# A graph-attention layer on one core: the first feed-forward product of each tile with the rows as weights, and its result turned back by TensorE

## The chip, the cores and the metric

One core of a Trainium2 chip runs the whole layer. The metric is the device time of one execution in microseconds. Five engines work in order of their own instructions and wait for each other on semaphores: TensorE (PE in the rows, its weight loads PEld), VectorE (DVE), ScalarE (ACT), GpSimd (POOL) and SyncE (SP).

## The reference, cut to what matters

`x` has 4096 rows of 512, and 131072 edges join them. The middle part, attention over the edges of each row, is computed by code that the change leaves as it is.

```python
def _ln(x, g, b): ...                     # layer norm
z = _ln(x, ln1_g, ln1_b)
att = _sparse_attention(z, row_index, col_index, att_bias, Wq, bq, Wk, bk, Wv, bv, Wo, bo)
x = x + att
z = _ln(x, ln2_g, ln2_b)
ff = jax.nn.silu(z @ W1 + b1) @ W2 + b2   # W1: 512 x 1024, W2: 1024 x 512
return x + ff                             # then one more norm of input + this
```

## The kernel before, in words

The first phase (about 1.9 ms of the profiled span) sorts the edges into records, computes q, k and v for all rows, and stores them. The second phase, where the change is, walks over 32 tiles of 128 rows (loop `tiles`, variable `t`). The edges of a tile are cut into groups of 8 per row, at least three groups per tile, 145 in all. GpSimd gathers the k and v rows of a group by eight indirect DMAs (L521) into a ring of three buffers, and SyncE passes their arrival on.

Each group goes through the engines as a pipeline. VectorE multiplies q and k (`products`, L991). TensorE sums the products by transposing matmuls (`sum_d`, L1321), adds up the v sums of the group before (`turn_sum`, L1349), and turns the scores (`turn_scores`, L1329, after ScalarE's copy in `take_scT`, L676). VectorE takes the maximum and subtracts it (`softmax`, L1037 to L1041), ScalarE takes the exponents (L687). The v rows are then weighed, half by ScalarE (`weigh`, L703: pair 3 of the group before ahead of the exponents, pair 0 behind them, with the copy `take_vT`, L682, in its middle) and half by VectorE (L1002). TensorE sums them (`sum_v`, L1339).

The order of instructions is written out by hand. The first three groups of a tile are stages 0, 1 and 2 on TensorE and VectorE, and all later groups share a loop, stage 3. ScalarE has one body for the first group (`body(t, None)`) and one for all others (`body(t, i)`). The feed-forward work of earlier tiles is threaded into these stages:

- TensorE, behind `sum_v(3)`: stage 0 has both halves of the second product, `down(oldest, 0)` and `down(oldest, 1)` (L1389), stage 1 has `up(older, 0)` (L1379) and `turn_att` (L1356), and stage 2 has `up(older, 1)` and the output projection `out_proj` (L1364). `turn_z2` (L1370) stands at the head of stage 1.
- ScalarE: `hidden(k, 0)` in the second group and `hidden(k, 1)` in the third, eight instructions each (L725 and L726 in turn).
- VectorE: `silu` (L1049) of half 0 in stage 2 and of half 1 in stage 0; the norm `middle` in stage 0 and the last norm in stage 2.

`up` makes the hidden layer already turned: W1 is the weight operand, 128 hidden units at a time, and the turned rows z2T stream through it, 128 columns. The result has a hidden unit on each partition, so b1 is one number per partition, and ScalarE adds it as the bias of its activations; and hT can at once be the weight operand of `down`. Each float32 matmul that is no transpose shows as two MATMUL records, so one half of `up` (16 matmuls) is 32 records and one half of `down` (4 matmuls of 512 columns) is 8 records. The hidden halves lie in the PSUM banks h_ps[0] and h_ps[1].

Of the kernel before, what the change touches and what calls it, by code (L numbers as in the profile page):

```python
# [14 lines left out]
P = 128  # L15
# [20 lines left out]
def layer_kernel(nc, x, src, dst, edge_bias, Wq, bq, Wk, bk, Wv, bv, Wo, bo, ln1_g, ln1_b,  # L36
# [30 lines left out]
    bias_rows = nc.dram_tensor("bias_rows", [3, 3 * C], BF16, kind="Internal").ap()  # L67
# [6 lines left out]
    with ExitStack() as ctx:  # L74
# [39 lines left out]
        def part(words):  # L114
# [14 lines left out]
        bias_c, bias_f, bias_r = (part(3 * KT).rearrange("p (w k) -> p w k", w=3) for _ in range(3))  # L129
        bias_cut = part(9 * KT // 2).bitcast(BF16).rearrange("p (i w k) -> p i w k", i=3, w=3)  # L130
# [27 lines left out]
        hT = part(HID)  # L158
        prods = part(GROUP * C).rearrange("p (s c) -> p s c", s=GROUP)
        vw = part(GROUP * C).rearrange("p (s c) -> p s c", s=GROUP)  # L160
        scT_sb, vT_sb = part(2 * P), part(C)
        assert max(used_sort, pos_c[0]) <= REGION_C
# [18 lines left out]
        b1_col = sb("b1_col", [P, HT])  # L181
        b1_half = sb("b1_half", [P, HT])
# [44 lines left out]
            att_sb wo_done z2_ready z2_turned z2_sb h_done0 h_done1 h_act0 h_act1 h_ready0 h_ready1 y_done y_taken out_ready out_sent consts_c  # L227
# [6 lines left out]
        H_DONE = [S["h_done0"], S["h_done1"]]  # L234
        LANDED = [S[f"landed{pair}"] for pair in range(PAIRS)]
# [28 lines left out]
        def _(sp):  # L264
# [10 lines left out]
            for w, b in enumerate((bq, bk, bv)):  # L275
                sp.dma_start(bias_c[:, w, :], b.rearrange("(p k) -> p k", p=P)).then_inc(S["weights_loaded"], 16)
            for to, b in ((bo_all, bo), (b2_all, b2)):
                sp.dma_start(to, b.rearrange("(a n) -> a n", a=1).broadcast_to([P, C])).then_inc(S["weights_loaded"], 16)
            with nc.allow_non_contiguous_dma(reason="vectors of a few KB to columns"):
# [3 lines left out]
                sp.dma_start(b1_col[:, :], b1.rearrange("(k p) -> p k", p=P)).then_inc(S["weights_loaded"], 16)  # L283
# [10 lines left out]
            with nc.allow_non_contiguous_dma(reason="pieces of three vectors, once"):  # L294
                sp.wait_ge(S["bias_cut"], 1)
                for w in range(3):
                    sp.dma_start(bias_rows[:, w * C:(w + 1) * C].rearrange("i (p k) -> p i k", p=P), bias_cut[:, :, w, :]).then_inc(S["bias_out"], 16)
# [4 lines left out]
            sp.wait_ge(S["bias_out"], 48)  # L302
            sp.dma_start(bias_bf, bias_rows).then_inc(S["bias_in"], 16)
# [297 lines left out]
        def _(act):  # L601
# [56 lines left out]
            act.mul(b1_half[:, :], b1_col[:, :], 0.5).then_inc(S["phase1_act"], 1)  # L658
            act.drain()
# [57 lines left out]
            def hidden(k, a):  # L717
# [56 lines left out]
            for a in range(2):  # L774
                hidden(NT, a)
# [718 lines left out]
```

## Time and profile before

| | |
|---|---|
| median of 3 timed runs | 3778.58 us (3778.52 to 3779.97) |
| span of the profiled execution, first to last instruction | 4385.0 us |
| second phase in it, 1900 to 4310 us | 2410 us, 145 groups |
| granted TensorE clock in it | 0.92 of full, against 0.65 in the first phase |
| share of the DMA engines in it | 0.72, 240 GB/s |

The profiled execution is 606 us (16%) longer than the timed ones, and the page gives no time for it beside its span. Durations of single instructions are read from it, and waits with caution. A group is measured here on TensorE, from the first L1329 row of one group to the first of the next.

### The profile page before, as it was taken

How to read it: one execution, taken by the hardware profiler on the slowest of the kernel's cores; microseconds unless marked ns; L12 is line 12 of the kernel's file. 1: busy time of each engine (PE TensorE's matmuls, PEld its weight loads, DVE VectorE, ACT ScalarE, POOL GpSimd, SP SyncE). 2: the span in 40 equal slices, each digit the busy share in tenths (PEclk: the TensorE clock that was granted, in tenths of full speed). 3: DMA queues.
4: the chain of work that ended last, by engine and by line, in shares of the span. 5: the costliest groups of instructions: out<-in, count | busy, mean ns of one | idle time of the engine just before them, and what ended most of it. 6: DMA issues, size and time to landing. Idle time of an engine off the chain costs nothing.

```text
span 4385.0 us, 82363 instructions
## 1 busy us (share of the span) xinstructions
PE 2962.7 (68%) x18693; PEld 2259.3 (52%) x18694; DVE 2634.4 (60%) x6428; ACT 1724.8 (39%) x6427; POOL 2648.6 (60%) x2550
## 2 busy tenths in 40 slices
PE   7444554455455455547778788888888888888888
PEld 5222222222222232236667676776767777677676
DVE  8555555455555555536567566666666666666665
ACT  0011111111111111125666565665666666566664
POOL 0255555555556555567667666666667667666662
PEclk5566666666666666668889999998999999999999
DMA  6222222222222222266667777777677777777762
GB/s 230 70 61 61 61 61 61 57 65 61 61 64 64 59 61 63 59 226 229 225 227 263 242 233 256 242 240 252 221 246 249 246 235 244 246 238 247 240 218 77
DMA packets 285667, 719.24 MB, mean 164 GB/s; under 512 B 86899, under 2 KB 103475, under 8 KB 285382
## 3 DMA queue, kind: packets, MB, share of 16 engines
q0 software_dynamic: 211776, 585.54, 40.9%
q1 hardware_dynamic: 73862, 133.41, 9.7%
q14 instruction: 22, 0.18, 0.0%
q8 instruction: 7, 0.11, 0.0%
HBM read 717.02 MB, written 72.97 MB: 180 GB/s over the span
## 4 chain that ended last, share of the span: by engine, by line
PE 37%; issue 18%; DVE 17%; another core or an unknown queue 14%; ACT 5%; DVEq 4%; POOL 2%; ACTq 1%; DMA 1%; POOLq 1%; PEld 0%; SPq 0%; PEldq 0%
PE bank L1321 10%; PE wide L1379 6%; PE wide L1339 6%; PE bank L1389 5%; ACT region_c L703 4%; DVE region_c L938 3%; DVE region_c L903 3%; PE bank L1278 2%; DVE region_c L914 2%; PE bank L1364 2%; DVE region_c L918 2%; PE bank L1220 2%; PE wide L1265 1%; DVEq L900 1%
## 5 line engine op out<-in xcount | busy, mean ns | idle before, releaser
L521 POOL DMA_INDIRECT region_a<-kv,cols x1160 | 1405.5, 1212 | 490.7 <-issue 451.2
L408 POOL DMA_INDIRECT records<-region_c,pos_i x1024 | 999.4, 976 | 895.9 <-DVE pos_i L921 588.5
L703 ACT ACTIVATE region_c<-region_a,pr 128x64 f32 x4640 | 1157.3, 337 | 96.1 <-remote 60.7
L991 DVE TENSOR_TENSOR region_c<-region_a,region_c 128x1024 f32 x580 | 674.4, 1221 | 233.4 <-issue 174.2
L1321 PE MATMUL bank<-ident,region_c 128*128 128x128 f32 x4640 | 614.1, 288 | 145.8 <-DVE region_c L991 89.1
L1321 PEld LDWEIGHTS bank<-ident,region_c 128*128 128x128 f32 x4640 | 581.4, 197 | 176.2 <-issue 163.8
L1339 PE MATMUL wide<-ident,region_c 128*128 128x128 f32 x4640 | 600.6, 287 | 67.3 <-ACT region_c L703 44.0
L1339 PEld LDWEIGHTS wide<-ident,region_c 128*128 128x128 f32 x4640 | 553.9, 151 | 96.5 <-ACT region_c L703 63.1
L914 DVE TENSOR_TENSOR region_c<-wide,region_c 128x512 f32<-128x512 f32 x128 | 136.3, 1065 | 700.3 <-remote 468.5
L1265 PE MATMUL wide<-region_c 64*128 64x64 f32 x2048 | 193.7, 345 | 461.8 <-issue 438.6
L1278 PE MATMUL bank<-region_b,region_a 128*128 128x512 f32 x768 | 495.9, 803 | 6.5 <-issue 6.1
L1265 PEld LDWEIGHTS wide<-region_c 64*128 64x128 f32 x2048 | 175.6, 251 | 551.6 <-issue 543.5
L1379 PE MATMUL wide<-region_c,region_b 128*128 128x128 f32 x2048 | 298.4, 303 | 107.7 <-issue 104.4
L1002 DVE TENSOR_TENSOR region_c<-region_a,pr 128x1024 f32<-128x1024 f32 x290 | 341.7, 1219 | 8.2 <-remote 6.7
L1379 PEld LDWEIGHTS wide<-region_c,region_b 128*128 128x128 f32 x2048 | 279.5, 217 | 120.4 <-issue 116.3
L1278 PEld LDWEIGHTS bank<-region_b,region_a 128*128 128x128 f32 x768 | 191.1, 262 | 273.1 <-issue 273.1
L647 ACT ACTIVATE region_a<-bank 128x512 f32<-128x512 f32 x96 | 57.3, 597 | 634.0 <-remote 419.5
L903 DVE SCALAR_TENSOR_TENSOR region_c<-region_a,region_c 128x128 bf16<-128x128 int16 x1024 | 291.7, 350 | 24.3 <-issue 24.3
L1389 PE MATMUL bank<-region_b,region_c 128*128 128x512 f32 x512 | 237.6, 607 | 21.6 <-issue 21.6
L676 ACT COPY region_c<-bank 128x256 f32<-128x256 f32 x145 | 53.9, 372 | 482.0 <-PE bank L1321 342.1
L1285 PE MATMUL bank<-ident,region_a 128*128 128x128 f32 x128 | 35.7, 434 | 289.5 <-DVE region_a L935 281.3
L1220 PE MATMUL bank<-region_c 128*64 128x64 bf16 x2048 | 189.8, 317 | 61.2 <-issue 34.3
(184 smaller groups left out, 3189.3 us busy)
## 6 DMA issues: line engine op xcount, KB each, us to landing
region_a<-srcT SPq DMA_DIRECT2D x128, 256.0 KB
region_a<-kv,cols POOLq DMA_INDIRECT x1160
region_a<-hiT SPq DMA_DIRECT2D x256, 64.0 KB
x_rows<-region_c SPq DMA_DIRECT2D x32, 512.0 KB
records<-region_c,pos_i POOLq DMA_INDIRECT x1024
kv<-region_a SPq DMA_DIRECT2D x32, 512.0 KB
records<-region_c SPq DMA_DIRECT2D x32, 480.0 KB, 14.8
region_a<-in_x_dram SPq DMA_DIRECT2D x32, 256.0 KB
```

The lines of the kernel that those rows point to most:

```text
L408: pool.indirect_dma_start(records, bass.IndirectOffsetOnAxis(ap=pos_i[j % 2][:, s:s + 1], axis=0), rec_w[j % 2][:, s, :], None).then_inc(S ...
L521: pool.indirect_dma_start(KV[r][:, s, :], None, kv, bass.IndirectOffsetOnAxis(ap=cols[r][:, s:s + 1], axis=0), bounds_check=L - 1, oob_is_ ...
L703: last = act.activation(vw[:, s, of], v_part[:, s, C + hd * D:C + (hd + 1) * D], ACT.Copy, scale=pr[:, s + 1, hd:hd + 1])
L903: last = dve.scalar_tensor_tensor(eq[:, s * P:(s + 1) * P], srcb[b][:, s * P:(s + 1) * P], src_f[:, bass.ds(st * STREAMS + s, 1)], tri[:, ...
L991: last = dve.tensor_tensor(prods[:, of, :], kv_in[:, of, 0:C], q.unsqueeze(1).broadcast_to([P, 2, C]), ALU.mult)
L1002: dve.tensor_tensor(vw[:, s:s + 2, :].rearrange("p s (h d) -> p s h d", h=HEADS), kv_in[:, s:s + 2, C:2 * C].rearrange("p s (h d) -> p s h ...
L1265: last = pe.matmul(wide_ps[b][:, side, s * LO:(s + 1) * LO], hitT[b][rows, s * P:(s + 1) * P], table_sb[rows, s * LO:(s + 1) * LO], start= ...
L1278: last = pe.matmul(qkv_ps[w][:, :], zT1[:, c * P:(c + 1) * P], Wqkv[:, w, c, :], start=False, stop=c == KT - 1)
L1321: last = pe.matmul(scT_ps[:, a * P:(a + 1) * P], prod_cols[:, i, a * SH:(a + 1) * SH], ident[:, :], start=i == 0, stop=i == D // FOLD - 1, ...
L1339: last = pe.matmul(vT_ps[:, c * P:(c + 1) * P], vw[:, s, c * P:(c + 1) * P], ident[:, :], start=s == 0 and c == 0, stop=s == GROUP - 1, is ...
L1379: last = pe.matmul(h_ps[m // 4][:, (m % 4) * P:(m % 4 + 1) * P], W1_sb[:, c, m * P:(m + 1) * P], z2T[:, c * P:(c + 1) * P], start=c == 0, ...
L1389: last = pe.matmul(y_ps[:, :], hT[:, m * P:(m + 1) * P], W2_sb[:, m, :], start=m == 0, stop=m == HT - 1)
```

## The change

`up` takes the turned rows z2T as weights, 128 at a time, and W1 streams through in 512 columns, so a half is 4 matmuls. The result has the rows on the partitions and the hidden units along the free axis. The bias b1 now varies along the free axis: it is cut into three bf16 rows whose sum is exactly b1, in the first phase beside the other biases, and enters by one more matmul with a bf16 weight of ones, three rows deep. ScalarE handles a half in two instructions of 512 columns (a halving copy, and tanh) instead of eight of 128. VectorE's `silu` is as before. Since `down` needs the hidden units on the partitions, TensorE turns each half by four transposes into the same PSUM bank (`turn_hidden`), and ScalarE copies it out. Two stages of semaphores are new: `h_turned` and `hT_sb`. `down` waits for `hT_sb` instead of `h_ready`.

```diff
 # ScalarE
-                for c in range(HT // 2):
-                    ps = h_ps[a][:, c * P:(c + 1) * P]
-                    half_b = b1_half[:, a * HT // 2 + c:a * HT // 2 + c + 1]
-                    act.activation(hT[...], ps, ACT.Identity, bias=half_b, scale=0.5)
-                    last = act.activation(ps, ps, ACT.Tanh, bias=half_b, scale=0.5)
-                last.then_inc(H_ACT[a], 1)
+                act.activation(hid[:, a * HID // 2:(a + 1) * HID // 2], h_ps[a][:, :], ACT.Copy, scale=0.5)
+                act.activation(h_ps[a][:, :], h_ps[a][:, :], ACT.Tanh, scale=0.5).then_inc(H_ACT[a], 1)
+            def turn_hidden(k, a):
+                act.wait_ge(H_TURNED[a], k)
+                act.copy(hT[:, a * HID // 2:(a + 1) * HID // 2], h_ps[a][:, :]).then_inc(HT_SB[a], 1)
...
                 weigh(0, at, now, t, i is None)
+                if i is None:
+                    with act.If(t > 2):
+                        turn_hidden(act.snap(older), 0)
+                        turn_hidden(act.snap(older), 1)
 # TensorE
-                for m in range(a * HT // 2, (a + 1) * HT // 2):
-                    for c in range(KT):
-                        last = pe.matmul(h_ps[m // 4][:, (m % 4) * P:(m % 4 + 1) * P], W1_sb[:, c, m * P:(m + 1) * P],
-                                         z2T[:, c * P:(c + 1) * P], start=c == 0, stop=c == KT - 1)
+                of = slice(a * HID // 2, (a + 1) * HID // 2)
+                pe.matmul(h_ps[a][:, :], ones_bf[:, :], b1_rows[:, of], start=True, stop=False)
+                for c in range(KT):
+                    last = pe.matmul(h_ps[a][:, :], z2T[:, c * P:(c + 1) * P], W1_sb[:, c, of], start=False, stop=c == KT - 1)
                 last.then_inc(H_DONE[a], 1)
+            def turn_hidden(k, a):
+                pe.wait_ge(H_READY[a], k)
+                for c in range(HT // 2):
+                    last = pe.transpose(h_ps[a][:, c * P:(c + 1) * P], hid[...], ident[:, :])
+                last.then_inc(H_TURNED[a], 1)
             def down(k, a):
-                pe.wait_ge(H_READY[a], k)
+                pe.wait_ge(HT_SB[a], k)
...
                         with pe.If(t > 2):                    # stage 0, behind sum_v(3)
                             pe.reg_add(oldest, oldest, 1)
-                            down(pe.snap(oldest), 0)
+                            turn_hidden(pe.snap(oldest), 1)
                     with pe.If(t > 2):
-                        down(pe.snap(oldest), 1)
+                        down(pe.snap(oldest), 0)
...
                 if stage == 1:                                # behind sum_v(3)
+                    with pe.If(t > 2):
+                        down(pe.snap(oldest), 1)
                     with pe.If(t > 1):
                         up(pe.snap(older), 0)
...
                         out_proj(t)                           # stage 2
+                    with pe.If(t > 1):
+                        turn_hidden(pe.snap(older), 0)
```

In the first phase SyncE issues one more small DMA out to `bias_rows` and one more in (the load of b1 itself is only laid out otherwise), VectorE's seven instructions that cut the biases work on 20 columns instead of 12, and ScalarE's halving of b1 is gone. Behind the loop the last three tiles get the same steps written out.

## Rows read from the trace of the kernel before

**Rows 1.** The page: span, and busy time of each engine.
```profile
span 4385.0 us, 82363 instructions
PE 2962.7 (68%) x18693; PEld 2259.3 (52%) x18694; DVE 2634.4 (60%) x6428; ACT 1724.8 (39%) x6427; POOL 2648.6 (60%) x2550
```
**Rows 2.** The page: the chain that ended last, share by engine.
```profile
PE 37%; issue 18%; DVE 17%; another core or an unknown queue 14%; ACT 5%; DVEq 4%; POOL 2%; ACTq 1%; DMA 1%; POOLq 1%; PEld 0%; SPq 0%; PEldq 0%
```
**Rows 3.** PE's timeline, a stage 0: start, length, line; idle before in brackets.
```profile
3280.99 0.63 PE L1329 MATMUL bank<-fold,region_c 128*128 128x32 f32 x4 [0.46 <-ACT region_c L676]
...
3285.74 7.03 PE L1389 MATMUL bank<-region_b,region_c 128*128 128x512 f32 x16
3292.61 0.60 PE L1370 MATMUL bank<-ident,region_c 128*128 128x128 f32 x4
...
3297.71 0.63 PE L1329 MATMUL bank<-fold,region_c 128*128 128x32 f32 x4 [0.46 <-ACT region_c L676]
```
**Rows 4.** PE's timeline, a stage 1.
```profile
3369.98 3.74 PE L1379 MATMUL wide<-region_c,region_b 128*128 128x128 f32 x32
3373.55 0.60 PE L1356 MATMUL bank<-ident,region_c 128*128 128x128 f32 x4
...
3378.65 0.63 PE L1329 MATMUL bank<-fold,region_c 128*128 128x32 f32 x4 [0.46 <-ACT region_c L676]
```
**Rows 5.** Stretches: length; busy of PE, PEld, DVE, ACT, POOL; clock; DMA share; GB/s.
```profile
1900.00:4310.00 2410.00, 1933.46 (x13198) 1657.10 (x13199) 1546.82 (x2777) 1463.41 (x5646) 1638.09 (x1506) 0.92 0.72 240
3281.00:3297.70 16.70, 15.71 (x92) 11.40 (x92) 14.23 (x32) 10.34 (x40) 13.04 (x13) 1.00 0.83 288
3365.20:3378.70 13.50, 12.47 (x109) 12.05 (x109) 10.35 (x16) 11.58 (x45) 10.41 (x10) 1.00 0.66 200
4263.70:4280.50 16.80, 15.67 (x112) 13.01 (x112) 12.01 (x24) 11.03 (x44) 12.25 (x13) 1.00 0.93 335
```
**Rows 6.** VectorE's timeline in the stage 0 of Rows 3.
```profile
3289.46 4.63 DVE L991 TENSOR_TENSOR region_c<-region_a,region_c 128x1024 f32 x4 [0.37 <-issue]
```
**Rows 7.** Groups in 1900:4300: busy us, mean ns; idle before, releasers.
```profile
L1379 PE MATMUL wide<-region_c,region_b 128*128 128x128 f32 x1856 | 276.0, 306 | 104.6 <-issue 104.4
L1389 PE MATMUL bank<-region_b,region_c 128*128 128x512 f32 x464 | 216.5, 609 | 21.6 <-issue 21.6
L1364 PE MATMUL bank<-region_b,region_c 128*128 128x512 f32 x240 | 115.8, 627 | 0.0
L725 ACT ACTIVATE region_c<-wide,b_half 128x128 f32<-128x128 f32 x232 | 88.5, 382 | 26.2 <-PE wide L1379 20.9 <-remote 5.2
L726 ACT ACTIVATE wide<-wide,b_half 128x128 f32<-128x128 f32 x232 | 83.2, 358 | 0.0
```
**Rows 8.** The first phase's bias matmul (L1276): duration ns min, median, max.
```profile
L1276 PE MATMUL bank<-region_c,ones_bf x96: 384/602/605, 172.2 to 1880.8; 3*128 3x512 bf16 x96
```
**Rows 9.** ScalarE's timeline in a stage 2 that nothing disturbs.
```profile
4267.57 0.26 ACT L687 ACTIVATE pr<-sc 128x72 f32<-128x72 f32 x1
...
4269.99 0.56 ACT L682 COPY region_c<-wide 128x512 f32<-128x512 f32 x1
4270.46 2.02 ACT L703 ACTIVATE region_c<-region_a,pr 128x64 f32 x8
```
**Rows 10.** PE's timeline after a long idle stretch.
```profile
3024.93 1.06 PE L1329 MATMUL bank<-fold,region_c 128*128 128x32 f32 x4 [2.69 <-ACT region_c L676]
3025.80 6.38 PE L1339 MATMUL wide<-ident,region_c 128*128 128x128 f32 x32
```
**Rows 11.** Stretches: the one of Rows 10.
```profile
3024.90:3032.20 7.30, 7.27 (x38) 7.28 (x39) 5.23 (x7) 6.08 (x25) 2.55 (x2) 0.56 0.38 151
```
**Rows 12.** ScalarE's timeline in the stage 0 of Rows 3.
```profile
3285.33 2.02 ACT L703 ACTIVATE region_c<-region_a,pr 128x64 f32 x8 [0.23 <-issue]
3292.82 0.58 ACT L682 COPY region_c<-wide 128x512 f32<-128x512 f32 x1 [5.48 <-remote]
```
**Rows 13.** Stretches: a disturbed stage 2.
```profile
3447.20:3473.10 25.90, 20.09 (x112) 17.33 (x112) 12.84 (x27) 11.07 (x44) 15.44 (x17) 0.80 0.76 264
```

More of the change, by code:

```diff
@@ L66, in layer_kernel @@
     row_key = nc.dram_tensor("row_key", [L], F32, kind="Internal").ap()
-    bias_rows = nc.dram_tensor("bias_rows", [3, 3 * C], BF16, kind="Internal").ap()
+    bias_rows = nc.dram_tensor("bias_rows", [3, 3 * C + HID], BF16, kind="Internal").ap()
     q_rows = nc.dram_tensor("q_rows", [L, C], F32, kind="Internal").ap()
@@ L128, in layer_kernel @@
         bias_bf = part(3 * C // 2).bitcast(BF16)[0:3, :]
-        bias_c, bias_f, bias_r = (part(3 * KT).rearrange("p (w k) -> p w k", w=3) for _ in range(3))
-        bias_cut = part(9 * KT // 2).bitcast(BF16).rearrange("p (i w k) -> p i w k", i=3, w=3)
+        bias_c, bias_f, bias_r = (part(3 * KT + HT) for _ in range(3))
+        bias_cut = part(3 * (3 * KT + HT) // 2).bitcast(BF16).rearrange("p (i k) -> p i k", i=3)
         bo_all, b2_all, xb_row = part(C), part(C), part(2 * C)
@@ L157, in layer_kernel @@
         s_all, z2 = part(2 * C), part(C)
-        hT = part(HID)
+        hid = part(HID)
+        hT = hid
         prods = part(GROUP * C).rearrange("p (s c) -> p s c", s=GROUP)
@@ L161, in layer_kernel @@
         scT_sb, vT_sb = part(2 * P), part(C)
+        b1_rows = part(HID // 2).bitcast(BF16)[0:3, :]
+        assert used_sort <= pos_c[0] - HID // 2
         assert max(used_sort, pos_c[0]) <= REGION_C
@@ L768, in _ @@
             take_vT()
+            for a in range(2):
+                turn_hidden(NT - 2, a)
             turn_z2(NT - 1)
@@ L772, in _ @@
             hidden(NT - 1, 1)
+            for a in range(2):
+                turn_hidden(NT - 1, a)
             turn_z2(NT)
@@ L775, in _ @@
                 hidden(NT, a)
+            for a in range(2):
+                turn_hidden(NT, a)
         @block.vector
@@ L878, in _ @@
             dve.drain()
-            dve.tensor_copy(bias_cut[:, 1, :, :], bias_r)
+            dve.tensor_copy(bias_cut[:, 1, :], bias_r)
             dve.drain()
-            dve.tensor_copy(bias_f, bias_cut[:, 1, :, :])
+            dve.tensor_copy(bias_f, bias_cut[:, 1, :])
             dve.drain()
@@ L1456, in _ @@
             turn_sum()
+            turn_hidden(NT - 2, 1)
             down(NT - 2, 0)
@@ L1463, in _ @@
             out_proj(NT)
+            turn_hidden(NT - 1, 0)
+            turn_hidden(NT - 1, 1)
             down(NT - 1, 0)
@@ L1468, in _ @@
             up(NT, 1)
+            turn_hidden(NT, 0)
+            turn_hidden(NT, 1)
             down(NT, 0)
```

33 lines of the change are left out of this document (17 added, 16 removed).

## The prediction, as put on record before the changed kernel was run

> **What bounds the kernel now.** I read the page first for which engine is busy: TensorE, with 68% of the span, and no other above 60% [rows 1]. The chain that ended last runs mostly through TensorE, then through waits that the profile calls issue, and VectorE [rows 2]. An average doesn't say what one more microsecond on TensorE costs, so I read the timeline of single groups. In a stage 0, from one L1329 row to the next (16.72 us), TensorE goes from `sum_v` into both halves of `down` without a gap, 6.87 us from 3285.74 to 3292.61, and from there into `turn_z2` [rows 3]. In a stage 1, `up(0)` takes 3.57 us and `turn_att` follows at once; the group is 13.4 us long [rows 4]. TensorE is busy 15.71 of 16.70, 12.47 of 13.50 and 15.67 of 16.80 us in undisturbed stages 0, 1 and 2 [rows 5]. So in these three stages TensorE's own queue is the bound, and feed-forward work put into it moves the next group's scores by nearly its own length. VectorE is the next limit in stage 0 only: its products end at 3289.46 + 4.63 = 3294.1, some 3.6 us ahead of the next L1329 [rows 3, 6]. The gathers have room: 0.72 of the DMA engines over the phase, though up to 0.93 in single stages [rows 5].
>
> **TensorE's instructions.** `up` before: 32 records in 3.57 us per half [rows 4]. After: 8 records of 512 columns. `down` has the same form and takes 6.87 / 2 = 3.44 us per half [rows 3]; so the columns cost what they cost, four times as many in a fourth of the records, and only 0.13 us go. The bias matmul is 512 columns of bf16. It appears only in the first phase, with a shortest record of 384 ns [rows 8]. A float32 record of 512 columns is 609 ns long [rows 7] at a pace of 430 ns, so 180 ns of a record overlap the next; that leaves 0.2 us (bounds: 0, fully overlapped, and 0.6, its longest record). `turn_hidden` is 4 transposes; `turn_z2` of the same form takes 3293.05 - 3292.61 = 0.44 us (its end is the next start, and I take the same for `turn_att`). Per tile: 2 x (3.44 + 0.2 - 3.57) + 2 x 0.44 = +1.0 us, bounds 0.6 to 1.8.
>
> Here the Trainium skill speaks for a better exchange. "TensorE: Matmul & The Clock Gate", section "Back-to-back issue gap", gives sustained 81 ns for a matmul of 128 columns and 131 ns for one of 512, that is 0.40 of the time for the same columns. By that the new `up` would cost 2 x 0.4 x 3.57 = 2.9 us instead of 6.9, and the sum below would be some 116 us (29 x 4.0) lower, about 3845 us and still slower than before. The trace disagrees: 430 ns against 3.57 / 32 = 112 ns [rows 3, 4], a ratio of 3.9, no saving in kind.
>
> **What moves on TensorE.** `down(1)` leaves stage 0 and goes to stage 1. Stage 1 was bound by TensorE, so it grows by 3.44 + 0.07 = 3.5 us. Stage 2 grows by `turn_hidden(0)` and the bias, 0.44 + 0.07 = 0.5 us. `turn_hidden(0)` waits for `silu(0)`, which VectorE does ahead of the scores of stage 2, so it doesn't stall.
>
> Stage 0 loses 3.44 us of `down(1)` and has 0.44 of `turn_hidden(1)`, but `down(0)` now waits for a copy by ScalarE. ScalarE issues that copy behind `weigh(0)`, and that stands behind the exponents of this same group, which need TensorE's own scores of this group. From the L1329 row of an undisturbed group (4263.7, the start of the last stretch of rows 5): exponents at 4267.57, that is +3.9, `take_vT` at +6.3, its second eight L703 end at 4270.46 + 2.02, +8.8 [rows 5, 9]. The copy is like L682, 0.56 us [rows 9]: +9.3, with the branch and the semaphore +9.5. TensorE is through with `sum_v` at +4.75 (3285.74 - 3280.99) and with the turn at +5.2 [rows 3]: it stands idle for 4.3 us. `down(0)` then ends at +12.95, where both halves ended at +11.62 before: stage 0 grows by 1.3 us although half its feed-forward work left. Queued behind the waiting `down(0)` on TensorE are `turn_z2` and `sum_d` of the next group, for which ScalarE and then VectorE wait. Bounds of this term: -1.0 (if the copy came in time, VectorE would hold the group, with the 3.6 us of rows 6 less the 2.5 us that `sum_d`, copy and scores take behind it) and +1.3.
>
> **The clock.** A gap on TensorE has a second price. Behind the 2.69 us gap at 3024.93, 32 records of L1339 took 6.38 us, where 32 of L1379 with the same shape take 3.74 [rows 4]; the granted clock in that stretch is 0.56, that is, mostly the 1.2 GHz level instead of 2.4 [rows 10, 11]. I looked at all 28 gaps over 2 us in the second phase: 26 of them are followed by work that is 1.2 to 3.3 us late, and the eight over 3 us by 2.4 us on average. I take 2.3 us per tile; bounds 0 and 3.4 (all of `down(0)` at half pace).
>
> **The other engines.** ScalarE had 16 instructions of L725 and L726 per tile, 382 and 358 ns each [rows 7]. The new ones are 2 halving copies of 512 columns (0.56 each [rows 9]), 2 tanh of 512 (between that and 4 x 0.36 = 1.4; I take 0.6) and 2 copies: 3.4 us against 5.9, so some 2.5 us are freed, at pace rather 1. ScalarE isn't late where it is freed: in stage 1 `hidden(0)` comes 3.5 us later because `up(0)` does, and still ends ahead of the next `take_scT`. I count nothing for it. If that cover is gone the loss is under 1 us a tile. VectorE's silu has the same form. The additional first-phase DMAs and the wider bias cut stand in a prologue, once: 2 small DMAs, up to 5 us if they end last, taken as 1.
>
> **The sum.** The wait is in 29 tiles (t > 2). Per tile 1.3 + 2.3 (stage 0) + 3.5 (stage 1) + 0.5 (stage 2) = 7.6 us. Some of it is taken back: in stages 3 TensorE waits for products of data that has to land, and with 0.83 to 0.93 of the DMA engines busy in calm stages [rows 5] later scores let the gathers catch up. I take 1.4 us a tile (bounds 0 and 4, the larger if gathers nearly bind the timed run). 29 x 6.2 = 180 us. Behind the loop three tiles are worked off serially with both turns ahead of `down(0)`; each lasts one ScalarE copy, one turn and the tail of a half longer, about 2 us, 6 together. Total +187: against the profiled span 4385.0 -> 4572. The profiled execution is 606 us longer than the median; the undisturbed stages on which the sum rests should be those of the timed run, so I carry the difference over whole: 3778.6 + 187 = 3966 us.
>
> **Rivals.**
>
> *A, the forecast: order bound.* TensorE's queue and the late copy, 3966 us; with the bounds of clock (0 to 3.4), take-back (0 to 4) and turns, 3890 to 4040. For it: stages without gaps on TensorE [rows 3 to 5].
>
> *B, the copy is later still.* In the stage 0 of rows 3 ScalarE stands idle for 5.48 us ahead of `take_vT` [rows 12], in the middle of `weigh(0)`, with a releaser that the profile doesn't know; this is so in every such group from t = 2 on. Before, nothing waited for it. After, the copy, and so `down(0)`, comes 5.5 us later: 29 x 5.5 = +160, 4125 us. Against it: the same code shows no such idle in the first tiles, the idle time ends a fixed 3.36 us after VectorE's L991 starts (3292.82 - 3289.46) [rows 6, 12], so it seems to hang on what the profiled VectorE does, and the timed runs are 606 us shorter.
>
> *C, hidden by the gathers.* If the timed run is close to bound by transfers (0.93 in a calm stage [rows 5]), TensorE's 6 us a tile mostly replace waits for data. With 4 to 5 us taken back instead of 1.4: 3778.6 + 29 x 1.5 + 6 = 3828 us. Against it: VectorE's and GpSimd's stretches in those stages show data in time.
>
> *D, faster: the dense narrow stream is what stops the core.* In a disturbed stage 2 the group takes 25.9 us instead of 16.8, at a clock of 0.80 [rows 5, 13], and TensorE's idle time for "issue" ahead of L1379 is 104.6 us, against 21.6 for L1389 and none for L1364, which stream equal columns in a fourth of the records [rows 7]. If the 64 records with their weight loads, 112 ns apart, cause this in timed runs too, the change takes up to 29 x 9.1 = 264 us away: 3966 - 264 = 3702 us. It decides from 6.4 us per tile on. Against it: stage 1 streams the same L1379 without a stall [rows 4], and the excess of the profiled execution over the timed ones is itself the size of these stalls.
>
> **Chances and range.** A 0.64, B 0.14, C 0.12, D 0.07, and 0.03 for cases that cancel. A difference under about 0.2% (7.6 us) can't be told from no change. Faster takes D; same takes the 0.03; slower is A, B and C, 0.90. The likeliest case gives 3966. For 8 in 10 I reach into C and B: 3845 to 4110.
>
> **What would show it.** In the profile after: L1379 in 8 float32 records a half, 430 ns apart, at about 3.4 us; in stage 0 an idle stretch of about 4.3 us on TensorE between four transposes and L1389, released by ScalarE's copy; a granted clock below full behind it; stage 1 at about 17 us where it was 13.4, stage 2 at about 17.3 where it was 16.8. Wrong would be: `down(0)` starting within 1 us of the turn (then the wait is covered), a clock that stays at full over the gap (the 2.3 falls away, 67 us), stage 2 without its stalls and shorter than before (D), or VectorE's L991 waiting for data in most groups (C).

## The result, and the profile after

The changed kernel takes 3891.36 us (median of 4 runs, 3877.54 to 3908.04) against 3779.27 for the kernel before in the same set: ratio 1.0293, 95% interval [1.0272, 1.0314]. It is 112 us slower; 187 were forecast, and 3891 lies in the stated range.

One thing has to be said before any number is compared. The kernels ran in sets, each on one chip, and the sets fall into two kinds; all runs of a set agree with each other. On the chips of the timed runs above, and of experiments 7 and 8, before takes 3779 us. On those of experiments 1 to 6 and 9 it takes 4401 to 4459 us, and the profile of before in [rows 1 to 13], with its 4385.0 us, is of that kind too. The profile of after is of the 3779 kind, from the fastest of its four runs. I call them the faster and the slower chips, though the sets of known chip were each on another one (6, 11 and 3 slower, 14 faster), so whether it is the chip or its state at that time isn't shown. I compare only within a kind, except where undisturbed stages are the same on both.

The page of after, with the lines that answer to [rows 1, 2, 7] (L1411 is `down`, L1395 the new `up`, L706 `weigh` on ScalarE):
```profile
span 3875.7 us, 79825 instructions
...
PE 2926.1 (75%) x17477; PEld 2071.4 (53%) x17478; DVE 2621.7 (68%) x6428; ACT 1681.6 (43%) x6106; POOL 2663.6 (69%) x2550
...
PE 32%; issue 19%; POOL 19%; ACT 10%; DVE 8%; DMA 7%; ACTq 3%; DVEq 2%; POOLq 1%; SPq 0%; PEld 0%; PEldq 0%
...
L706 ACT ACTIVATE region_c<-region_a,pr 128x64 f32 x4640 | 1155.1, 337 | 33.6 <-issue 33.6
...
L1411 PE MATMUL bank<-region_b,region_c 128*128 128x512 f32 x512 | 283.3, 707 | 112.2 <-ACT region_c L731 112.2
...
L1395 PE MATMUL wide<-region_b,region_c 128*128 128x512 f32 x512 | 240.2, 612 | 0.0
```
`down` now waits 112.2 us for L731, ScalarE's copy; that is 3.9 us in each of 29 tiles, and its mean record is 707 ns where it was 609 [rows 7]. Before, this line never waited for another engine [rows 7], and in no_turn (experiment 7) its idle time is 0.0.

TensorE's timeline in after, a stage 0 and the stage 1 behind it (start, length, line; idle time before in brackets), the answer to [rows 3, 4]:
```profile
3377.28 0.63 PE L1344 MATMUL bank<-fold,region_c 128*128 128x32 f32 x4 [0.46 <-ACT region_c L679]
...
3382.03 0.60 PE L1402 MATMUL wide<-ident,region_c 128*128 128x128 f32 x4
3386.55 5.40 PE L1411 MATMUL bank<-region_b,region_c 128*128 128x512 f32 x8 [3.91 <-ACT region_c L731]
3391.78 0.60 PE L1385 MATMUL bank<-ident,region_c 128*128 128x128 f32 x4
...
3396.89 0.63 PE L1344 MATMUL bank<-fold,region_c 128*128 128x32 f32 x4 [0.46 <-ACT region_c L679]
...
3401.64 3.60 PE L1411 MATMUL bank<-region_b,region_c 128*128 128x512 f32 x8
3405.18 0.39 PE L1393 MATMUL wide<-region_c,ones_bf 3*128 3x512 bf16 x1
3405.49 3.70 PE L1395 MATMUL wide<-region_b,region_c 128*128 128x512 f32 x8
3409.03 0.60 PE L1371 MATMUL bank<-ident,region_c 128*128 128x128 f32 x4
...
3414.13 0.63 PE L1344 MATMUL bank<-fold,region_c 128*128 128x32 f32 x4 [0.46 <-ACT region_c L679]
```
The reader should see three things. The idle 3.91 us ends with ScalarE's copy. The same 8 records of `down` take 5.23 us behind it (3386.55 to 3391.78; 5.27 in the mean of the 29 tiles) and 3.54 in stage 1, where nothing stood still ahead of them. And stage 1 holds a half of `down` that was not there before. ScalarE's timeline shows what the copy stands behind:
```profile
3381.13 0.26 ACT L690 ACTIVATE pr<-sc 128x72 f32<-128x72 f32 x1
3381.62 2.02 ACT L706 ACTIVATE region_c<-region_a,pr 128x64 f32 x8 [0.23 <-issue]
3383.55 0.56 ACT L685 COPY region_c<-wide 128x512 f32<-128x512 f32 x1
3384.01 2.01 ACT L706 ACTIVATE region_c<-region_a,pr 128x64 f32 x8
3385.93 1.04 ACT L731 COPY region_c<-wide 128x512 f32<-128x512 f32 x2
```
ScalarE stands still for only 0.23 us from the exponents (L690) to the copy (L731): it is in the order that the code gives it. The 5.48 us of [rows 12] are not there.

Stretches of after, with the columns of [rows 5]: the stages 0, 1 and 2 of this tile, then `down(0)` behind the gap, then `down(1)`.
```profile
3377.30:3396.90 19.60, 14.69 (x89) 10.95 (x89) 14.49 (x33) 11.31 (x42) 14.56 (x15) 0.91 0.81 275
3396.90:3414.10 17.20, 16.23 (x93) 11.42 (x93) 9.37 (x14) 10.40 (x39) 13.19 (x13) 1.00 0.67 213
3414.10:3431.40 17.30, 16.27 (x94) 11.58 (x94) 12.56 (x27) 10.02 (x38) 9.10 (x10) 1.00 0.78 257
...
3386.60:3391.80 5.20, 5.20 (x9) 2.13 (x10) 5.20 (x6) 0.37 (x1) 3.95 (x4) 0.67 0.92 345
3401.70:3405.20 3.50, 3.50 (x10) 1.31 (x9) 3.50 (x4) 3.50 (x15) 3.20 (x2) 1.00 0.69 239
```
The granted clock is 0.67 behind the gap, a mix of the 1.2 and the 2.4 GHz level, and 1.00 without one.

For the experiments I added up the stages of each trace: a stage lasts from one turn of the scores (L1329 of before, L1344 of after) to the next; there are 31, 31, 30 and 52 of stages 0 to 3.

```
sum of the stages, us       stage 0  stage 1  stage 2  stage 3    all
faster chips: no_turn         607.4    426.5    505.0    620.2   2159.1
              row_bias        555.4    457.5    537.0    619.2   2169.1
              after           598.6    526.4    517.7    615.9   2258.6
slower chips: before_again    605.2    493.8    707.2    611.5   2417.7
              down1_moved     591.9    602.5    608.0    629.5   2431.9
              before_b        638.5    504.3    659.7    630.8   2433.3
              after_b         851.0    603.1    548.9    618.6   2621.6
              early_copy_b    605.9    589.0    596.7    637.0   2428.6
              both_back_b     833.1    488.1    558.5    641.8   2521.5
              three_slots     551.8    454.6    755.9    625.2   2387.5
```
The first phase ends at 1532 to 1533 us in the three traces of the faster chips, so all of the change's cost is behind it. On the slower ones it ends at 1937 to 1974 us: some 400 to 440 us of their 620 to 680 us more lie in a phase that no version changes. On those chips the same kernel's sums differ by up to 48 us a stage from one trace to another (before_again and before_b), so a smaller difference there means little.

### The profile page after: what moved, and what is told of

It reads as the page before. It is cut to its first block, busy times and chain, and to the rows that moved or that the text cites. A ratio compares the mean times of both kernels' runs of the same rounds, so it can differ in the third digit from the quotient of the medians.

```text
span 3875.7 us, 79825 instructions
## 1 busy us (share of the span) xinstructions
PE 2926.1 (75%) x17477; PEld 2071.4 (53%) x17478; DVE 2621.7 (68%) x6428; ACT 1681.6 (43%) x6106; POOL 2663.6 (69%) x2550
## 4 chain that ended last, share of the span: by engine, by line
PE 32%; issue 19%; POOL 19%; ACT 10%; DVE 8%; DMA 7%; ACTq 3%; DVEq 2%; POOLq 1%; SPq 0%; PEld 0%; PEldq 0%
POOL records L412 15%; PE bank L1336 11%; ACT region_c L706 9%; PE bank L1411 7%; PE wide L1395 6%; DMA records<-region_c,pos_i 5%; POOL region_a L525 3%; PE bank L1379 3%; DVE region_c L1006 2%; PE wide L1354 2%; DVE region_c L953 2%; ACTq L706 2%; PE wide L1364 1%; PE bank L1235 1%; DVE region_c L838 1%
## 5 line engine op out<-in xcount | busy, mean ns | idle before, releaser
L525 POOL DMA_INDIRECT region_a<-kv,cols x1160 | 1414.7, 1220 | 427.6 <-issue 373.0
L412 POOL DMA_INDIRECT records<-region_c,pos_i x1024 | 1011.4, 988 | 485.2 <-issue 292.2
L706 ACT ACTIVATE region_c<-region_a,pr 128x64 f32 x4640 | 1155.1, 337 | 33.6 <-issue 33.6
L1006 DVE TENSOR_TENSOR region_c<-region_a,region_c 128x1024 f32 x580 | 675.6, 1220 | 211.9 <-SPq L370 109.6
L1354 PE MATMUL wide<-ident,region_c 128*128 128x128 f32 x4640 | 572.8, 277 | 75.5 <-ACT region_c L706 75.5
L1354 PEld LDWEIGHTS wide<-ident,region_c 128*128 128x128 f32 x4640 | 521.8, 145 | 108.4 <-ACT region_c L706 108.4
L1293 PE MATMUL bank<-region_b,region_a 128*128 128x512 f32 x768 | 481.4, 785 | 0.0
L630 ACT COPY region_c<-region_a 128x64 f32 x128 | 32.4, 253 | 1033.4 <-DMA records<-region_c,pos_i 1033.4
L1411 PE MATMUL bank<-region_b,region_c 128*128 128x512 f32 x512 | 283.3, 707 | 112.2 <-ACT region_c L731 112.2
L1411 PEld LDWEIGHTS bank<-region_b,region_c 128*128 128x128 f32 x512 | 110.3, 226 | 244.7 <-issue 125.3
L1395 PE MATMUL wide<-region_b,region_c 128*128 128x512 f32 x512 | 240.2, 612 | 0.0
L936 DVE TENSOR_TENSOR pos_i<-region_c 128x8 int32<-128x8 f32 x128 | 21.4, 167 | 273.6 <-DMA records<-region_c,pos_i 268.8
L1025 DVE TENSOR_TENSOR wide<-wide,pr 128x512 f32<-128x512 f32 x113 | 78.3, 693 | 176.1 <-PE wide L1364 176.1
```

What stands on the lines that cost most here:

```text
L412: pool.indirect_dma_start(records, bass.IndirectOffsetOnAxis(ap=pos_i[j % 2][:, s:s + 1], axis=0), rec_w[j % 2][:, s, :], None).then_inc(S ...
L525: pool.indirect_dma_start(KV[r][:, s, :], None, kv, bass.IndirectOffsetOnAxis(ap=cols[r][:, s:s + 1], axis=0), bounds_check=L - 1, oob_is_ ...
L706: last = act.activation(vw[:, s, of], v_part[:, s, C + hd * D:C + (hd + 1) * D], ACT.Copy, scale=pr[:, s + 1, hd:hd + 1])
L1006: last = dve.tensor_tensor(prods[:, of, :], kv_in[:, of, 0:C], q.unsqueeze(1).broadcast_to([P, 2, C]), ALU.mult)
L1293: last = pe.matmul(qkv_ps[w][:, :], zT1[:, c * P:(c + 1) * P], Wqkv[:, w, c, :], start=False, stop=c == KT - 1)
L1354: last = pe.matmul(vT_ps[:, c * P:(c + 1) * P], vw[:, s, c * P:(c + 1) * P], ident[:, :], start=s == 0 and c == 0, stop=s == GROUP - 1, is ...
```

## Experiments

**1. before_again: the kernel before, unchanged, profiled again.**

> The kernel of before, unchanged: a second profiled execution, since the first took 4385.0 us where the timed runs take 3779. Theory: the extra time of the first is one of the execution, and this profile comes near 3779 us, with its second phase made of tiles like the calmest of the first (stage 0 near 16.7 us, stage 1 near 13.4, stage 2 near 16.8); the change's own differences by stage can then be read as after minus this one: +2.9, +3.8 and +0.5 us, 7.2 us x 29 tiles = 207 us, of which the timed runs show only 112, so some 95 us have to come back in stage 3 or in tiles where before waits for its gathers. Rival: the first profile shows what always happens under the profiler, and this one is again near 4385 us.

4450.19 us, in a set where before took 4458.97 (median of 19). The rival holds as far as it goes: the first profile was no accident. But it isn't the profiler either; the timed runs of this set are as slow.

**2. early_copy and early_copy_b: the copy of half 0 ahead of the exponents.**
```
 # ScalarE, after weigh(3)
+if i is None: with act.If(t > 2): turn_hidden(older, 0)
 exponents()
 weigh(0, ...)
-    turn_hidden(older, 0)
     turn_hidden(older, 1)
```


> The kernel after, with ScalarE's copy of half 0 of the turned hidden layer taken up ahead of the stage's exponentials; the copy of half 1 stays where it is. Theory (the order bound of the prediction): down(0)'s wait of 3.9 us for that copy is what makes stage 0 of after 19.6 us instead of 16.7, so it goes, and TensorE's granted clock no longer falls behind it; the copy's 0.6 us now stand before the exponentials. Stage 0 comes to 16 to 17 us, and the time falls by 2.9 to 3.5 us x 29 = 85 to 100 us, to 3790 to 3805. Rival B (ScalarE's place in the chain is what counts, since the copy has its cost wherever it stands): the exponentials come 0.7 us later and with them all of stage 0; the gain is under 30 us. Rival C (gathers bound the tiles anyway): what stage 0 gives up, stage 3 takes as a wait for rows; the time stays within 0.5% of after.

> The kernel after with ScalarE's copy of half 0 ahead of the exponentials, again: on the other chip its stage 0 had fallen to 16.7 us at the calm tiles, stages 1 and 2 stood at 17.24 as in after. Theory on a chip where before takes 3779 us: 19.6 - 16.7 = 2.9 us x 29 = 84 us below after, about 3807. Rival (gathers take it back in stage 3): within 30 us of after.

Both sets met slower chips: 4461.04 us, 0.9988 [0.9953, 1.0023] of before, and 4455.71 us, 1.0022 [1.0001, 1.0043]. In the second set after itself ran (experiment 5) and took 4640.27, so one moved copy takes 185 us away, twice what I expected, and that is nearly all of the 199 us that the change costs there. TensorE's timeline of early_copy_b, a stage 0 (L1405 is the turn, L1414 `down`, L1388 `turn_z2`), then ScalarE's:
```profile
4298.54 0.63 PE L1347 MATMUL bank<-fold,region_c 128*128 128x32 f32 x4 [0.46 <-ACT region_c L679]
...
4303.29 0.60 PE L1405 MATMUL wide<-ident,region_c 128*128 128x128 f32 x4
4303.73 3.60 PE L1414 MATMUL bank<-region_b,region_c 128*128 128x512 f32 x8
4307.16 0.60 PE L1388 MATMUL bank<-ident,region_c 128*128 128x128 f32 x4
```
```profile
4302.21 0.57 ACT L731 COPY region_c<-wide 128x512 f32<-128x512 f32 x1
4302.86 0.26 ACT L690 ACTIVATE pr<-sc 128x72 f32<-128x72 f32 x1
```
`down(0)` follows the turn at once and has its full pace again, 3.43 us, at a granted clock of 1.00. The next scores come at 4315.25, a stage of 16.71 us, as before [rows 3]. The idle time and the slow clock go together when their cause goes. Rival B of the expectation (the copy costs wherever it stands) is out: the exponents come 4.32 us into the stage, 0.47 later than in after, and the stage is no longer for it. What the move is worth on a faster chip was not seen.

**3. fill_gap: the gap filled with 32 transposes.**
```
 with pe.If(t > 2):
+    pe.wait_ge(y_taken, oldest)
+    for n in range(32): pe.transpose(y_ps[...], ident, ident)
     down(oldest, 0)
```


> The kernel after, with 32 more transposes of the identity into y's bank ahead of down(0) in stage 0, where TensorE waits 3.9 us for ScalarE: 32 x 0.11 us = 3.6 us of work that leaves the wait's end where it is. Theory of the prediction: 2.3 us a tile of the change's cost are the granted clock's fall behind that gap; with the gap filled the clock stays at full and the time falls by up to 2.3 x 29 = 67 us. Rival: the clock's fall costs little (down(0)'s products are 0.43 us each at full clock and stage 1 is bound elsewhere); the time stays within 0.3% of after.

4659.45 us, 1.0439 [1.0382, 1.0496] of before, on a slower chip, where after without the fill stands at 1.0433 (experiment 5). The time did not fall by the 67 us (1.4%) of the theory; the two ratios are the same within their 0.6%, as the rival has it. The group of the added transposes in the 29 tiles:
```profile
L1438 PE MATMUL bank<-ident 128*128 128x128 f32 x928 | 188.2, 356 | 157.4 <-issue 157.0
```
The fill stood still itself, 157.4 / 29 = 5.4 us a tile with nothing to wait for, and lasted as long as the gap does there, so it isn't a clean test of the total. Of the pace it is one. With the fill ahead of it `down(0)` takes 3.56 us in the mean of 29 tiles (3.43 to 4.17), and behind the empty gap of after_b 5.66 (5.07 to 6.46). In the tile that I followed, the last 16 transposes of the fill and then `down(0)` show that the clock had fallen in the fill's own stops and came back before `down(0)` needed it (stretches as in [rows 5]):
```profile
4034.40:4037.70 3.30, 3.30 (x16) 3.17 (x16) 3.30 (x4) 3.06 (x11) 2.23 (x3) 0.50 0.94 353
4037.70:4041.60 3.90, 3.90 (x10) 1.75 (x9) 0.66 (x4) 0.40 (x1) 3.14 (x3) 0.89 0.57 168
```
So the slow pace is the gap's doing. What it costs in time is less than it looks: in the mean of the tiles `down(0)` ends 1.6 us earlier in the stage than in after_b (20.75 against 22.38), stage 0 is 0.8 us shorter, and the run is no faster.

**4. down1_moved: before, with only `down(.,1)` moved to stage 1.**
```
-    with pe.If(t > 2): down(oldest, 1)     # end of stage 0
 if stage == 1:
+    with pe.If(t > 2): down(oldest, 1)
     with pe.If(t > 1): up(older, 0)
```


> The kernel of before, with only down(.,1) moved from the end of stage 0 to the head of up(0) in stage 1. Theory of the prediction: stage 1 grows by down(1)'s 4 products of 0.43 to 0.86 us (up to 3.5 us) and stage 0 gives back only as far as VectorE lets it (about 1.1 us), so the move alone costs about 2.3 us x 29 = 67 us. Rival: TensorE bounds both stages; what stage 1 gains, stage 0 gives back, and the time stays within 0.3% of before.

4464.55 us, 1.0016 [0.9990, 1.0043]: nothing, on a slower chip. The forecast 67 us did not come; but the time stays by another way than the rival's. Against before_again stage 1 grew by 109 us (3.5 us x 31), stage 0 gave back only 13, stage 3 grew by 18, and stage 2 gave 99. There TensorE stands still ahead of L1379 without a cause that the trace names; before_again, then down1_moved, the waits of TensorE in the second phase:
```profile
PE wide L1379 <- issue: 98.0, 92, 2.4
```
```profile
PE wide L1379 <- issue: 43.3, 41, 1.9
```
On this kind of chip stage 2 has idle time that an addition in stage 1 seems to be paid from. The stalls don't only shrink, though: those of the same kind ahead of L1321, over all stages, rise from 48.3 to 110.9 us.

**5. before_b and after_b: both kernels, unchanged, in one set.**

> The kernel of before, unchanged, profiled once more. The first set of four ran on a chip on which before took 4459 us and its profile showed long waits for rows in stage 2 (mean 23.6 us for that stage, 16.8 at the least); the timed runs of the change stand at 3779. If this set meets a chip of the 3779 kind, its trace shows what a calm tile of before is there. Theory: stage 0 16.7 us, stage 1 13.4 to 13.9, stage 2 16.8; then after's 19.6, 17.2 and 17.2 stand 7.2 us above them a tile, 207 us in all, and the 112 measured need a stage of before that is longer than its least. Rival: before's stages are longer there than the least ones of the first profile (a short stage 1 is only had behind a late stage 2), and the sum of stages 0 to 2 differs from after's by no more than 112 / 29 = 3.9 us a tile.

> The kernel after, unchanged, in the same set as the others. On a chip where before takes 3779 us: 3880 to 3905. On one where before takes 4459: theory (the waits for rows there hide TensorE's order) the early copy alone was already at before's time, and after is at most 1% above before; rival (the wait for the copy stands in the chain there too): 4459 + 112, 2.5% above.

This set met a slower chip too, so before_b could not answer its question; no_turn does, in experiment 7. before 4441.56 us (13 runs), after_b 4640.27: 1.0433 [1.0408, 1.0459], +199 us. "At most 1% above" is wrong; the wait for the copy is in the chain on these chips, and longer. A stage 0 of after_b, first TensorE, then ScalarE:
```profile
4008.32 0.63 PE L1344 MATMUL bank<-fold,region_c 128*128 128x32 f32 x4 [0.46 <-ACT region_c L679]
...
4023.34 5.91 PE L1411 MATMUL bank<-region_b,region_c 128*128 128x512 f32 x8 [9.66 <-ACT region_c L731]
```
```profile
4012.66 2.02 ACT L706 ACTIVATE region_c<-region_a,pr 128x64 f32 x8 [0.23 <-issue]
4020.32 0.58 ACT L685 COPY region_c<-wide 128x512 f32<-128x512 f32 x1 [5.63 <-remote]
4020.80 2.02 ACT L706 ACTIVATE region_c<-region_a,pr 128x64 f32 x8
4022.72 1.04 ACT L731 COPY region_c<-wide 128x512 f32<-128x512 f32 x2
```
This is the mechanism of rival B of the prediction: ScalarE's 5.5 us idle time of [rows 12] stands ahead of the copy, and `down(0)` starts 15.0 us into the stage where B says 9.5 + 5.5. Over the 29 tiles TensorE waits for the copy (us, times, longest):
```profile
PE bank L1411 <- ACT region_c L731: 328.4, 29, 16.2
```
Stage 0 costs 213 us more than in before_b, stage 1 99 more, and stage 2, with its own stalls, gives 111 back.

**6. both_back and both_back_b: early copy, and `down(.,1)` back in stage 0.**
```
 # early_copy, and on TensorE, stage 0:
     down(oldest, 0)
+    down(oldest, 1)
 # stage 1:
-    down(oldest, 1)
```


> The kernel after with ScalarE's copy of half 0 ahead of the exponentials and down(.,1) back behind down(.,0) in stage 0. Theory (the order is the cost, the new product and the turning are nearly free): stage 1 gives back down(1)'s 3.4 us, stage 0 becomes about 17.9 us since TensorE now ends it (down(1) waits for the copy of half 1 at 9.6 us into the stage, ends at 13.1, then 4.5 us of transposes and sums up to the next turn of the scores); 2.1 us x 29 = 60 us below the early copy alone, and at 3779-us conditions within 50 us of before. Rival (the turning itself costs, by TensorE's added transposes, two bias products and ScalarE's two copies): it stays 60 us or more above before.

> The kernel after with ScalarE's copy of half 0 ahead of the exponentials and down(.,1) back in stage 0, a second time, for a chip on which before takes 3779 us (on the one before it stood 2.8% above before, with TensorE held for the copy of half 1, which there lay behind an idle time of ScalarE's of 5.6 us). Theory (the change's cost is where TensorE stands waiting for the copies and where the second product was put; the turning itself, its transposes, bias products and copies are nearly free): stages 0 to 2 come to about 17.9 + 13.9 + 17.2 = 49.0 us of TensorE's and VectorE's work, which is less than the 50.2 us a tile that the kernel without the turning took there with its wait for the output rows; so the time is within 0.5% of before. Rival (the copy of half 1 still holds TensorE): stage 0 at 19 us or more, 1% or more above before. On a chip of the other kind: again 2.5 to 3% above.

Slower chips both times: 4572.10 us, 1.0283 [1.0254, 1.0312], and 4550.31 us, 1.0339 [1.0314, 1.0365]. The first was forecast 60 us below the early copy alone and stands 116 above it, and the second is a little over the 2.5 to 3% that was said for such a chip. A stage 0 of the second:
```profile
4082.40 0.63 PE L1347 MATMUL bank<-fold,region_c 128*128 128x32 f32 x4 [0.46 <-ACT region_c L679]
...
4087.59 3.60 PE L1414 MATMUL bank<-region_b,region_c 128*128 128x512 f32 x8
4097.30 5.85 PE L1414 MATMUL bank<-region_b,region_c 128*128 128x512 f32 x8 [6.11 <-ACT region_c L731]
```
Half 0 is on time, and half 1 now waits 6.11 us for its copy, which lies behind ScalarE's idle time. In early_copy the same copy is as late and nobody is in need of it until stage 1. So `down(.,1)` in stage 1 is no mere loss: it hides its copy. What both_back does on a faster chip was not seen.

**7. no_turn: the new product without the turning** (no transposes, no copies back, `down` in its old places and released by VectorE).
```
-turn_hidden(...)                     # TensorE and ScalarE, all
 def down(k, a):
-    pe.wait_ge(HT_SB[a], k)
+    pe.wait_ge(H_READY[a], k)
```


> The kernel after without the turning of the hidden layer: no transposes and no copies back, down() in its old places and released by VectorE; the second product so works on numbers laid out the other way. What is left of the change is the first product with W1 streaming, the bias rows, and ScalarE's 2 instructions a half instead of 8. Theory (the cost of the change is the order and the copies, the new product is nearly free): within 0.5% of before, whichever kind of chip it is. Rival D of the prediction (the dense narrow stream of W1 stops holding the engine up, and ScalarE has 12 instructions fewer a tile): 0.7% or more faster than before, so that the turning eats a gain that is there. Third way (the product's wide form costs TensorE the time by itself): 0.7% or more slower.

3772.74 us against 3778.61 in its set, 0.9991 [0.9978, 1.0005]. The stages 0 to 2 of after stand 598.6 + 526.4 + 517.7 - 607.4 - 426.5 - 505.0 = 104 us above those of no_turn, 3.6 us a tile, which is what the rival of before_b's expectation said (at most 3.9). The new form of `up`, the bias rows and ScalarE's 12 fewer instructions a tile are worth nothing that can be measured. All of the 112 us are in the turning and the order it forces.

This is also the first trace of the old order on a faster chip, and stage 0 is not 16.7 us there but 19.6 on average. VectorE's and TensorE's timelines of such a stage, which begins at 3306.97:
```profile
3313.91 0.60 DVE L1097 TENSOR_SCALAR region_c<-region_c,mv,rstd 128x512 f32<-128x512 f32 x1
3317.65 0.69 DVE L1101 TENSOR_TENSOR region_c<-region_c 128x512 f32 x1 [3.14 <-DMA out_dram<-region_c,out_idx]
```
```profile
3318.59 0.60 PE L1374 MATMUL bank<-ident,region_c 128*128 128x128 f32 x4
3321.22 2.98 PE L1325 MATMUL bank<-ident,region_c 128*128 128x128 f32 x16 [2.02 <-DVE region_c L995]
...
3327.58 0.63 PE L1333 MATMUL bank<-fold,region_c 128*128 128x32 f32 x4 [0.46 <-ACT region_c L679]
```
`residual` (L1101) waits until the output rows of two tiles earlier have landed, since they leave from the slot that it writes. Why they land so late is in the same trace. VectorE has the rows ready at 3287.0, GpSimd issues their DMA only at 3311.92, behind the gathers that stand ahead of it in its order, and 5.7 us later they have landed:
```profile
3286.46 0.55 DVE L1069 TENSOR_SCALAR region_c<-region_c,mv,rstd  x1
```
```profile
3311.92 1.05 POOL L452 DMA_INDIRECT out_dram<-region_c,out_idx  x1 [0.30 <-issue]
```
In no_turn GpSimd issues this DMA 2.5 to 7.6 us behind the start of the stage 0 that waits for it; in after it does so for twelve tiles and from then on ahead of that start, and the wait is gone. The products, and then TensorE, are late by it, and TensorE is slow behind its own gap: the stage is 20.6 us long. The waits of VectorE for that landing (us, times, longest), in no_turn, row_bias and after:
```profile
DVE region_c L1101 <- DMA out_dram<-region_c,out_idx: 94.4, 28, 6.1
```
```profile
DVE region_c L1101 <- DMA out_dram<-region_c,out_idx: 55.0, 28, 5.5
```
```profile
DVE region_c L1112 <- DMA out_dram<-region_c,out_idx: 26.8, 12, 4.9
```

**8. row_bias: before, with the bias as rows and W1 still as weights** (ScalarE with 2 instructions a half).
```
 for m in ...:
+    pe.matmul(to, b1_rows[:, m * P:(m + 1) * P], ones_bf, start=True, stop=False)
     for c in range(KT): pe.matmul(to, W1_sb[:, c, m...], z2T[:, c...], start=False, ...)
```


> The kernel before with the bias of the first product brought in by TensorE alone: 8 more products a tile of a 3x128 bias row with ones, W1 still as weights, the hidden layer still comes out turned, ScalarE takes each half with 2 instructions of 512 instead of 8 of 128. Theory (ScalarE's hidden instructions are not in the chain): within 0.3% of before. Rival (a ScalarE instruction saved is a gain where its engine stops for 5 to 7 us a stage, as in the profiles of the first two sets): 0.5% or more faster than before, which would be the version to keep.

3779.31 us, 1.0005 [0.9995, 1.0014]: no gain. Against no_turn it shows what an addition to TensorE costs on a faster chip. Its 8 more products and narrow stream make stages 1 and 2 longer by 31 + 32 = 63 us, stage 0 gives 52 back, and the runs differ by 7 us. The wait for the landing is 39 us shorter. So in this pair the time added between one tile's stage 0 and the next is mostly paid out of that wait.

**9. three_slots: before, with a third slot for outgoing rows.**
```
-s_all, z2 = part(2 * C), part(C)
+s_all, z2 = part(3 * C), part(C)
-    hold(out_sent, sent); residual(...)          # VectorE, stage 0
+    residual(...)
+    hold(out_sent, sent); last_norm(...)         # stage 2
```


> The kernel before with a third slot for the rows on their way out, so that VectorE's residual in stage 0 no longer waits until the rows of two tiles earlier have landed; the wait moves to the last norm in stage 2, where the index of the rows is overwritten. In the kernel without the turning VectorE stood 94 us in 28 tiles for that landing, in the one with the row bias 55 us in 28, in after 27 us in 12: what the change adds to stages 1 and 2 is taken out of this wait, and that is why 7.2 us a tile by the least stages became 3.9. Theory (the wait is a bound of its own, set by the queue of gathers that the rows stand in): without it the stages fall to their least, 16.7 + 13.4 + 16.8, and the time falls by 60 to 95 us, 1.6 to 2.5%, where before takes 3779 us. Rival (the gathers bound the tile and the wait is only where it shows): the waits move to the arrival of rows in the other stages, and the time stays within 0.3%. On a chip of the other kind, where stage 2 waits 8 us longer anyway: within 0.5% by both.

4408.30 us, 1.0009 [0.9988, 1.0029], on a slower chip, as both theories have it for that kind: there before_b waits only 11.6 us for the landing in the whole run, and three_slots none. Whether the faster chips would gain is open. No version that ran beats before.

## Why the prediction came out as it did

The direction, the costs that A names and the range are right; the size is 75 us too high, and with 3891 the result lies at the lowest edge of A's own 3890 to 4040. Its steps, each against after's rows and the undisturbed stages of before:

- *`down(0)` held by the copy.* Forecast: start 9.5 us into the stage, 4.3 us idle. Measured 9.27 and 3.91. Right.
- *The clock behind the gap.* Forecast 2.3 us; 5.23 against 3.44 [rows 3] is 1.8, at 0.67. Right in kind, 0.5 too high. (The 28 gaps from which it was drawn are those behind 2200 us; the second phase of that trace has 40 over 2 us, 17 of them over 3.)
- *Stage 0* in all: forecast 1.3 + 2.3 = 3.6; measured 19.61 - 16.72 = 2.9.
- *Stage 1*: forecast 3.5; 17.24 - 13.4 = 3.8. *Stage 2*: forecast 0.5; 17.24 - 16.8 = 0.4.
- *TensorE's instructions.* The new `up` takes 3.54 us (3.44 forecast), the bias 0.31 (0.2), a turn 0.44: 2 x (3.54 + 0.31 - 3.57) + 0.88 = 1.4 us a tile where 1.0 was said. The 443 ns a record of the new `up` stand against the 131 that the Trainium skill has for a matmul of 512 columns in "TensorE: Matmul & The Clock Gate", section "Back-to-back issue gap": the measurement decides. (The prediction's "about 3845" by that page should read 3966 - 116 = 3850.)
- *Before take-back* that is 7.1 us a tile against 7.6, or 206 us, and 8 us behind the last group (83.7 us in after, 75.5 in no_turn) against 7 forecast there and in the first phase. The runs say 112.
- *The take-back is the term that was mis-sized*: 1.4 us forecast (bounds 0 to 4), (206 + 8 - 112) / 29 = 3.5 measured. Its place was wrong too. I put it in stage 3, where gathers could catch up; stage 3 of after and no_turn differ by 4 us in sum. It comes from stage 0: of no_turn's 94 us of waiting for the output rows, 68 are gone in after, and by the stage above, where 3.14 us of wait made 3.9 us of stage, that is some 84 us. I had read stages 0 only for their least length, 16.7 us, and taken every longer one for a disturbance of that execution. In that profile this is not far off; all its waits for the landing are these, so the term could hardly have been sized from it:
```profile
DVE region_c L1097 <- DMA out_dram<-region_c,out_idx: 6.9, 4, 2.4
```
  The pair no_turn and row_bias supports this cause; on the faster chips no run took the wait away, so it isn't shown by intervention.

Since that wait can swallow some 3 us a tile whatever adds them, the 112 us can't be divided between the late copy and the moved half. Stage by stage, after minus no_turn is -9, +100, +13 and -4 us, and +8 behind the last group: the late copy costs stage 0 nothing net, because the landing had cost it as much. That doesn't make it free: with stages 1 and 2 at 17.24, a stage 0 of 16.7 would be under what after has by 2.9 us, at most 84 us in all. That is an estimate that no run on a faster chip tested, and a high one: after still waits 26.8 us for the landing, mostly hidden under the late copy, and shorter tiles would bring more of it back.

- *Rival B* didn't happen in the timed runs: ScalarE has no such idle time in any of the three traces of the faster chips. On the slower ones it did in after_b: stage 0 grew by 213 us, between A's 29 x 3.6 = 104 and B's 104 + 160 = 264. But stage 2 gives back, and the whole is +199 where B says +347. That this is near A's +187 is luck: two large terms that A doesn't have nearly cancel.
- *Rival C* was nearer than its 3828, 63 us too low, makes it look. What swallows the cost is a wait for rows on their way out, not in, but one that GpSimd's gathers cause (experiment 7). And its sum has a slip: with 4 to 5 us taken back of 7.6 a tile stays 2.6 to 3.6, not 1.5, so C should have read 3778.6 + 29 x 2.6 + 6 = 3860 to 3889. The result is A's costs with nearly C's take-back.
- *Rival D* is out by no_turn on the faster chips. On the slower chips stage 2 is indeed 111 us shorter in after_b, but down1_moved, with the old narrow stream, loses 99 there too, so the form of the product isn't needed for it.
- *The difference carried over whole* from a profile 606 us longer than the timed runs: its reason (undisturbed stages are the same) held, the least stage 0 in the old order is 16.72 or 16.73 us on both kinds. What didn't hold is that the timed runs have nothing above the undisturbed stages. The kernel before itself has no trace on a faster chip; no_turn and row_bias, which take as long, stand for it, and as they wait 94 and 55 us for the landing, its own wait isn't known.

## What to carry to other kernels

When an operand is turned through another engine, look at where that engine's queue takes up the copy, not at what the copy costs: 0.56 us of ScalarE's time, queued behind its bulk work, became 3.9 us of idle TensorE and a lower clock behind it, and the one move ahead of the exponents took 185 us away where it was tried, on slower chips, where TensorE's wait was the longer one. Where a stage is longer than its least, look up what ends the wait in it, for such a wait can absorb what a change adds: here rows that were ready at 3287.0 and that GpSimd, behind its gathers, sent off at 3311.92. And where a profile's own time is far from the timed runs, forecast for both kinds of stage, or ask first which waits of it the timed runs can have.

## What the hardware showed that I had not expected

- The two kinds of chips: the same kernel takes 3779 or 4401 to 4459 us. The instructions are as long on both (1220 ns for VectorE's product of 128x1024, 337 for ScalarE's 128x64, in before_again and in after); what differs are idle times without a known cause, such as ScalarE's ahead of `take_vT`: 290.2 us in 51 places in before_b, none in after. More than half of the difference lies in the first phase. Why is open.
- On those chips stalls move from stage to stage with the code. 32 added transposes brought 5.4 us of standing still a tile with them.
- The price of a gap at TensorE grew little with its length: `down(0)` took 5.23 us behind 3.91 us and 5.75 behind 9.66 (4023.34 to 4029.09), against 3.5 without one; in the mean of 29 tiles 5.27 behind 3.9 us (after) and 5.66 behind 11.3 (after_b).
